# A depthwise-convolution block on one core: image 0's statistics taken alone, its high part formed straight from x, TensorE's ring taps given back to the vector engines

## The reference

```python
xd = jnp.concatenate([x[:, :, 0::2, 0::2], x[:, :, 0::2, 1::2], x[:, :, 1::2, 0::2], x[:, :, 1::2, 1::2]], axis=1)
feats = jnp.concatenate([_dwconv(xd, w1, 1), _dwconv(xd, w3, 3), _dwconv(xd, w5, 5)], axis=1)
y = jnp.einsum('bchw,oc->bohw', feats, w_proj[:, :, 0, 0])
...
x = x + _L0_conv_ref(_gn(x), L0_conv_w1, L0_conv_w3, L0_conv_w5, L0_conv_w_proj)
```

## Time and profile before

| | |
|---|---|
| time, median of 3 runs (lowest, highest) | 147.63 us (145.98, 148.36) |
| the profiled execution's own time | 147.7 us |
| its span, first to last instruction | 145.9 us |
| TensorE busy | 129.1 us (88% of the span) |
| VectorE busy | 119.8 us (82%) |
| ScalarE, POOL busy | 103.0 us (71%), 98.3 us (67%) |
| mean granted TensorE clock | 0.979 |

### The profile page before, as it was taken

The page is one execution under the profiler, slowest core; times in us unless marked ns, Lnnn a source line. Parts: engine busy times, 40 slices in busy tenths (PEclk is TensorE's granted clock), DMA queues, the critical chain, the costliest instruction groups (busy, mean ns, idle before and its releaser), DMA issues.

```text
span 145.9 us, 1480 instructions
## 1 busy us (share of the span) xinstructions
PE 129.1 (88%) x501; PEld 95.9 (66%) x501; DVE 119.8 (82%) x134; ACT 103.0 (71%) x110; POOL 98.3 (67%) x73
## 2 busy tenths in 40 slices
PE   0374699999999999999999999999999999999910
PEld 0222578788876777678767776777677867776600
DVE  0198999996299999999999999799938995999460
ACT  2285999999955999599959995999599950004100
POOL 7104799999699628994999399829993999100840
PEclk9999879999999999999999999999999999999996
DMA  3999993052043007000708699107094992853966
GB/s 101 216 210 212 209 211 50 0 110 49 0 98 57 0 19 136 0 4 17 136 0 180 122 186 206 38 17 136 0 216 84 174 198 55 180 112 85 196 145 150
DMA packets 35431, 15.73 MB, mean 108 GB/s; under 512 B 34016, under 2 KB 34144, under 8 KB 35040
## 3 DMA queue, kind: packets, MB, share of 16 engines
q1 hardware_dynamic: 33408, 8.39, 31.6%
q0 software_dynamic: 1440, 7.04, 24.9%
...
...
## 4 chain that ended last, share of the span: by engine, by line
PE 85%; DVE 4%; DMA 3%; ACT 2%; ACTq 1%; issue 1%; DVEq 1%; POOL 0%; POOLq 0%
PE YP L551 75%; PE YP L594 9%; DMA w_sb<-in_L_conv_w_dram 3%; DVE st L424 2%; DVE X L522 1%; ACT G L340 1%; DVE weff L449 1%; DVEq L86 0%; ACT HI L384 0%; PE SMALL L533 0%; POOL rstd L253 0%; ACTq L312 0%; ACTq L311 0%; PE SMALL L539 0%; ACTq L310 0%
## 5 line engine op out<-in xcount | busy, mean ns | idle before, releaser
L275 POOL TENSOR_TENSOR RING_SUM<-RING_SUM,PROD 128x900 f32<-128x900 f32 (+1 forms) x37 | 75.2, 2034 | 7.7 <-ACT PROD L365 3.8
L489 DVE SCALAR_TENSOR_TENSOR ACC<-G,coef,ACC 128x930 f32<-128x930 f32 (+1 forms) x64 | 76.6, 1197 | 2.0
L551 PE MATMUL YP<-HI,whi 128*128 128x512 f32 (+1 forms) x150 | 39.1, 413 | 2.8 <-ACT HI L384 2.8
L551 PE MATMUL YP<-LO,whi 128*128 128x512 f32 (+1 forms) x150 | 40.4, 420 | 0.0
L551 PE MATMUL YP<-HI,wlo 128*128 128x512 f32 (+1 forms) x150 | 37.7, 402 | 0.0
L551 PEld LDWEIGHTS YP<-HI,whi 128*128 128x128 f32 x150 | 29.5, 197 | 11.0 <-DVE whi L468 3.4
L365 ACT ACTIVATE PROD<-G,coef 128x900 f32<-128x900 f32 (+1 forms) x37 | 36.2, 1053 | 0.0
L551 PEld LDWEIGHTS YP<-LO,whi 128*128 128x128 f32 x150 | 28.5, 190 | 10.0 <-issue 3.4
L551 PEld LDWEIGHTS YP<-HI,wlo 128*128 128x128 f32 x150 | 28.3, 190 | 7.1
L375 ACT ACTIVATE Y<-YP 64x1024 f32<-64x1024 f32 x14 | 15.3, 1096 | 24.1 <-PE YP L594 23.9
L340 ACT ACTIVATE G<-X,nbias,rstd 64x1024 f32<-64x1024 f32 (+2 forms) x18 | 21.9, 1215 | 1.9 <-DVE nbias L442 1.5
...
## 6 DMA issues: line engine op xcount, KB each, us to landing
...
X<-in_x_dram SPq DMA_DIRECT2D x12, 256.0 KB, 5.4
...
out_dram<-X SPq DMA_DIRECT2D x12, 256.0 KB, 5.8
...
w_sb<-in_L_conv_w_dram ACTq DMA_DIRECT2D x1, 12.5 KB, 3.8
```

Source lines behind the costliest of these rows:

```text
L275: pool.tensor_tensor(dst, dst, prod(b, k), ALU.add).then_inc(prod_added, 1)
L489: dve.scalar_tensor_tensor(part(ACC, tap), g_tap(b, tap), of5(tap), part(ACC, tap), ALU.mult, ALU.add).then_inc(acc_step, 1)
L551: mm = nc.tensor.matmul(dst, w[:, n, :], src, start=start, stop=False, skip_group_check=True)
```

## The change

Parts, in the order of the program:

- **x is also loaded in another layout** (XS: each channel's 64x64 cut into 4 parts of 16 rows, one per partition) for images 0 and 1. VectorE takes their statistics from XS (`part_bn`), spreads them with a mask (L485), TensorE sums the four parts by a 0/1 matrix `same` (`sum_parts`), VectorE aggregates (`part_variance`, `part_bias`). Image 0 and image 1 now have statistics of their own; pairs 1 to 3 go as before, at other places of `between`, their powers on POOL at other places too.
- **The high part of image 0 straight from x**: three quarter-to-half pieces on ScalarE (`high_half`, L377), one on VectorE (L547); G follows on ScalarE (L387).
- **Weights in three chunks of three taps**, with (0, 0) last; six taps are scaled on ScalarE, three on POOL (L329); VectorE adds and casts per chunk, POOL forms wlo per chunk (L333). The 3x3 coefficients are loaded through POOL's queue as its first instruction. Zero pads are cleared by VectorE instead of POOL. `coef` is copied by ScalarE.
- **No ring taps on TensorE**: VectorE has 10, 10, 11, 10, ... taps (before 8, 11, 11, 10, ...), POOL's products are 5, 5, 4, 5, ... (before 4, 4, 4, 5, ...).
- **copy_y(b-2) among the products of image b** instead of copy_y(b-3) before the normalisation of image b.
- **Other keep-warm matmuls**: 9 of 128 columns before the transposes, 3 behind them, 8 of 512 columns behind `sum_parts(0)`.

```diff
-EXTRA = [(1, 2), (-1, 2), (1, -2)]
-EXTRA_OF = {0: EXTRA}
 POOL_TAPS = [(0, 2), (-2, -2), (-2, 2), (2, -2), (2, 2), (-2, -1), (2, 1)]
-POOL_N = [5, 5, 5, 6, 6, 6, 6, 6]
+POOL_N = [6, 6, 5, 6, 6, 6, 6, 6]
...
+INV_STD_AT = {(3, 2): 2, (5, 2): 3}
...
-WARM = (2, 2)
+WARM = (9, 3, 8)
+COPY_Y_AT = [0, 0, 0, 1, 3, 3, 3, 3]
...
+        def load_parts(eng, b, c0, c1, s):
+            src = x[b].rearrange("c (k r) w -> (c k) (r w)", k=PARTS)
+            eng.dma_start(XS[:, b, c0:c1], src[:, c0:c1]).then_inc(s, 16)
         @block.sync
         def _(sp):
-            load_x(sp, 0, x_top, 0, PH // 2)
-            load_x(sp, 0, x_loaded[0], PH // 2, PH)
-            for t in range(1, PAIRS):
-                load_x(sp, t, x_loaded[t], 0, PH)
+            load_parts(sp, 0, 0, 512, xs_loaded[0])
+            load_parts(sp, 0, 512, 1024, xs_loaded[1])
+            load_image(sp, 0, image_loaded[0])
...
+            pool.dma_start(w_sb[:, W3_AT:W1_AT], w3.rearrange("c a h w -> c (a h w)")).then_inc(w3_loaded, 16)
...
+            for n in range(ACT_SCALED, N_INNER):
+                pool.tensor_scalar(weff[:, n, :], wpT[:, 2, :], of5(INNER[n]), None, ALU.mult).then_inc(pool_scaled, 1)
+            for k in range(CHUNKS):
+                taps = slice(k * CHUNK, (k + 1) * CHUNK)
+                pool.wait_ge(whi_ready, k + 1)
+                pool.tensor_tensor(wlo[:, taps, :], weff[:, taps, :],
+                                   whi[:, taps, :].bitcast(F32), ALU.subtract).then_inc(wlo_ready, 1)
+            low_image(0)
             inv_std(2, 1, 2)
-            for b in range(1, B):
-                sum_ring(b)
-                if b == 1:
-                    inv_std(3, 2, PAIRS)
+            sum_products(0)
+            low_image(1)
+            inv_std(3, 2, 3)
+            sum_products(1)
...
+            def high_half(r0, r1, j, done):
+                src = X[0:HALF, 0, r0:r1, :].rearrange("p h (w j) -> p h w j", j=2)[:, :, :, j]
+                act.activation(s_image(HI, 0, r0, r1)[HALF * j:HALF * (j + 1)], src, ACT.Identity,
+                               bias=nbias[0:HALF, 0:1], scale=rstd[0:HALF, 0:1]).then_inc(done, 1)
...
+                    if b >= 2 and k == COPY_Y_AT[b]:
+                        copy_y(b - 2)
...
+            high_half(0, TOP, 0, hi_top)
+            high_half(TOP, PH, 0, hi_bottom)
+            high_half(TOP, PH, 1, hi_ready)
+            normalise(0, 0, PH, g_ready)
...
+                dve.wait_ge(part_stats, 2 * b + 3)
+                dve.tensor_tensor(spread[:, b, :, :], stp[:, b, None, :].to_broadcast([P, PARTS, STATS]),
+                                  mask[:, :, None].to_broadcast([P, PARTS, STATS]), ALU.mult).then_inc(spread_done, 1)
+            def part_variance(b):
+                dve.wait_ge(spread_summed, b + 1)
+                dve.bn_aggr(agg1[:, b, :], SPREAD_PS[b]).then_inc(agg1_done, 1)
+                dve.wait_ge(agg1_done, b + 1)
+                dve.tensor_scalar(vare[:, b:b + 1], agg1[:, b, 1:2], EPS, None, ALU.add).then_inc(stat_step, 1)
+            def part_bias(b):
+                dve.wait_ge(rstd_done, b + 1)
+                dve.scalar_tensor_tensor(nbias[:, b:b + 1], agg1[:, b, 0:1], -1.0, rstd[:, b:b + 1],
+                                         ALU.mult, ALU.mult).then_inc(stats_ready, 1)
...
-            between = {(0, 0): lambda: aggregate(1), (0, 2): lambda: (bn(2), aggregate(2)), (0, 3): lambda: variance(2, 1, 2),
-                       (0, 4): lambda: bn(3), (0, 6): lambda: aggregate(3), (0, 5): lambda: bias(2, 1, 2),
-                       (0, 7): lambda: variance(3, 2, PAIRS), (1, 5): lambda: bias(3, 2, PAIRS)}
+            between = {(0, 0): lambda: part_variance(1), (0, 2): lambda: part_bias(1), (0, 3): lambda: bn(1),
+                       (0, 4): lambda: aggregate(1), (0, 5): lambda: variance(1, 1, 2), (0, 6): lambda: bias(1, 1, 2),
+                       (1, 9): lambda: bn(2), (2, 0): lambda: aggregate(2), (2, 5): lambda: variance(2, 2, 3),
+                       (2, 7): lambda: bias(2, 2, 3), (3, 9): lambda: bn(3), (4, 0): lambda: aggregate(3),
+                       (4, 5): lambda: variance(3, 3, 4), (4, 7): lambda: bias(3, 3, 4)}
...
+            for _ in range(WARM[0]):
+                keep_warm(ident[:, :], P)
...
+                nc.tensor.matmul(SPREAD_PS[b], same[:, :], spread[:, b, :, :].rearrange("p k s -> p (k s)"),
+                                 start=True, stop=True).then_inc(spread_summed, 1)
...
+                if b in (0, 2, 4):
+                    t = b // 2 + 1
+                    combine(t, t, t + 1)
...
             for _ in range(WARM[1]):
-                keep_warm()
-            pe.wait_ge(whi_ready, 1)
+                keep_warm(ident[:, :], P)
+            pe.wait_ge(w5_loaded, 16)
+            pe.wait_ge(w3_loaded, 16)
+            coefficients(0, W1_AT, coef_ready)
+            sum_parts(0)
+            pe.wait_ge(low_zero, 1)
+            zeros = LO[:, SLOTS - 1, :]
+            for _ in range(WARM[2]):
+                nc.tensor.matmul(YP[:, 0, 0:512], zeros[:, 0:P], zeros[:, 0:512], start=True, stop=True)
```

More of the change, by code:

```diff
@@ L52 @@
 TOP = BANK_ROWS + 1
-WARM = (2, 2)
+WARM = (9, 3, 8)
+COPY_Y_AT = [0, 0, 0, 1, 3, 3, 3, 3]
+CHUNK = 3
+CHUNKS = N_INNER // CHUNK
+ACT_SCALED = 6
+PARTS = 4
+STATS = 12
+COLS = 2 + PAIRS - 1
 SUMS = 3
@@ L232, in _ @@
                                base=0, pattern=[[-1, P]], channel_multiplier=1).then_inc(const_step, 1)
+            pool.memset(same[:, :], 0.0).then_inc(stat_const, 1)
+            for k in range(PARTS):
+                pool.wait_ge(stat_const, k + 1)
+                v = same[:, :].rearrange("p (n c) -> p n c", c=C)
+                pool.affine_select(out=v, in_=v, compare_op=ALU.not_equal, fill=1.0, base=-k,
+                                   pattern=[[0, P // C], [-PARTS, C]], channel_multiplier=1).then_inc(stat_const, 1)
             a = avg[:, :].rearrange("p (b i c) -> p b i c", b=2, i=2)
@@ L340, in normalise @@
                     act.activation(g_image(b, r0, r1)[HALF * j:HALF * (j + 1)], rows[:, :, :, j], ACT.Identity,
[L341 to L342 removed]
+                                   bias=nbias[p0:p0 + HALF, col(b):col(b) + 1],
+                                   scale=rstd[p0:p0 + HALF, col(b):col(b) + 1]).then_inc(done, 1)
             def split(b):
@@ L452, in _ @@
+            part_bn(0)
+            part_variance(0)
             dve.wait_ge(wpT_ready, 3)
             dve.wait_ge(coef_copied, 1)
-            bn(0, 0, 2)
             add_w3(0, 1, 2)
-            bn(0, 2, 4)
-            aggregate(0)
-            add_w3(3, 4)
-            variance(1, 0, 1)
-            add_w3(5, 6)
-            bias(1, 0, 1)
-            add_w3(7, 8)
-            dve.scalar_tensor_tensor(weff[:, 0, :], wpT[:, 0, :], coef[:, W1_AT:W1_AT + 1],
-                                     weff[:, 0, :], ALU.mult, ALU.add).then_inc(weff_step, 1)
@@ L471, in add_tap @@
+            cast_w(2)
+            part_bn(1)
             def add_tap(b, k):
@@ L525, in _, with keep_warm @@
         def _(pe):
-            pe.wait_ge(const_step, 4)
+            def keep_warm(tile, n):
+                nc.tensor.matmul(YP[:, 0, 0:n], tile, tile, start=True, stop=True)
+            pe.wait_ge(const_step, 3)
+            for _ in range(WARM[0]):
+                keep_warm(ident[:, :], P)
             for k in range(3):
@@ L578, in low @@
                     mm = tap_matmuls(b, n, whi, LO)
-                extra = EXTRA_OF.get(b, [])
-                if extra:
-                    pe.wait_ge(extra_low_ready, 1)
-                for tap in extra:
-                    n = PE_TAPS.index(tap)
-                    tap_matmuls(b, n, whi, HI)
-                    tap_matmuls(b, n, wlo, HI)
-                    mm = tap_matmuls(b, n, whi, LO)
                 mm.then_inc(inner_done, 1)
+                if b in (0, 2, 4):
+                    t = b // 2 + 1
+                    combine(t, t, t + 1)
             def ring(b):
```

261 lines of the change are left out of this document (152 added, 109 removed).

## The result

| | median | range | runs |
|---|---|---|---|
| before | 146.91 us | 145.98 to 148.36 | 4 |
| changed | 148.47 us | 148.16 to 148.97 | 4 |

The ratio is 1.011, 95% interval 1.006 to 1.016: 1.1% slower, more than the noise and less than 2%. The profiled execution took 148.97 us (span 147.2), that of before 147.7. In some executions a kernel falls into a slower state, and every ratio here compares the other executions alone, while the medians are over all.

What follows compares the result with a forecast made beforehand. TensorE bounds the kernel before and gains about 5 us, but the bound moves to VectorE: its ledger puts F(7) at 137.9 and ring(7) at 138.0 instead of 137.23, +0.8 on 147.7, so 148.5 us, range 144.1 to 150.9.

Steps and rivals of the forecast that it cites:

- Case A: The main case, with holds and waits as summed: 148.5 us, with its tails 147.6 to 150.9, chance 0.42.
- The head: Start of the kernel: transposes at 6.6 us, G(0) ready at 16.3, third cast ending at 17.3.
- case D: POOL's weight scalings take t instead of 0.35 us, shifting the first ring tap by 3(t - 0.35); 151.6 at 1.4, chance 0.10.
- case B: Spreading of image 1 gets in before POOL's low part, first ring tap at 18.7 instead of 20.8: 146.4 us, chance 0.20.
- The spreading: VectorE's two-SBUF-input spreading of image 1 starts 0.2 us behind POOL's low part and waits 2.2; first ring tap at 20.8.
- Pair 1's power: POOL has it done at 35.0 us, VectorE asks at 32.6 and waits 2.3; F(0) at 39.6.
- Image 2's first step: VectorE's step meets POOL's first add of image 3: a hold of 0 or 1.9 us, taken as 0; F(2) at 69.5.
- Image 6: VectorE starts image 6 at 112.9 us, 3.4 after F(5), because pair 3's bias comes late; F(7) at 137.9.
- What follows is unchanged: After ring(7), four matmuls, two adds and the last stores take as long as before, so its 0.8 us delay sets the end.
- The copies of Y cost nothing: ScalarE's copies among the products cost nothing, as ScalarE waits for biases anyway; a late copy could take TensorE 1 to 2 us.
- case C: No holds between VectorE and POOL in the head, F(0) 3.6 us earlier: 144.9, or 144.2 with the clock early; chance 0.24.
- VectorE trails TensorE by 1.06 us only: Before the change, F(7) is done at 136.17 and its product starts at 137.23, so TensorE's gain needs VectorE's ring to gain too.

Runs made afterwards that it cites:

- e10: Changed kernel with ScalarE scaling all nine weights and POOL none: 146.56 us, 0.997 of the kernel before.
- e3: Changed kernel with image 1's spreading on ScalarE, as four scaled copies between products of image 0: 146.60 us, 0.992 of the kernel before.
- e2: Changed kernel with each image's spreading as four VectorE instructions of one tensor input instead of one with two: 149.23 us, 1.013 of the kernel before.
- e4: Changed kernel with pair 1's power on POOL behind its fourth product add of image 0: 148.97 us, 1.010 of the kernel before.
- e11: Changed kernel with many follow-up edits together, but pair 1's power at its old place: 142.91 us, 0.973; with that power moved too, 141.06 us.
- e9: Changed kernel with the copies of Y back at their place of before, three images behind: 152.31 us, 1.040 of the kernel before.
- e5: Kernel before with only image 0's ring taps off TensorE, POOL taking one tap more of images 0 and 1: 144.63 us, 0.983.
- e6: Changed kernel with pair 3's statistics, combination and bias earlier: 147.12 us, 0.998 of the kernel before.

## Why the prediction was right, and where it was not

The forecast was 148.5 us in 144.1 to 150.9, and the median is 148.47. Case A happened. So good an agreement is in part luck. The sum was made for the profiled execution, which took 148.97 us, 0.5 over it. That execution was the slowest of the four. The base was off too: the forecast takes 147.63 us for the kernel before, and with its fourth run the median is 146.91. So the change was forecast at 0.6% and measured at 1.1%. Inside the sum two errors of 1.5 us cancel (below).

- **The bound moves to VectorE**: right (chain, and 5.2 us of TensorE's waits for F in all, 2.34 of them before ring(7)).
- **The head**: transposes at 6.96 instead of 6.6 (nine products 4.21 for 4.05, and a start at 2.96 for 2.5); G(0) at 16.5 (16.3); third cast ends at 16.96 (17.3). POOL's scalings took 0.63, not 0.35: a part of case D, whose 3(t - 0.35) is 0.8 us. e10 shows 0.7 for the cast; the other 2.1 of its first ring tap are case B's race, which that edit won through a later G.
- **The spreading**: 2.28 us, ending with POOL's low part, first tap at 20.39 (20.8). e3 shows that the end hangs on it, with 2.8 us; e10, in which the cast came earlier too, gained 2.1. Its explanation was too narrow (e2).
- **Pair 1's power**: wait 2.36 (2.3), F(0) at 39.8 (39.6). That this wait was on the path was true only in the sum, not as a cause: removed alone it gives nothing (e4), removed with the rest 2.2 us (e11).
- **Image 2's first step** is the term of the sum that was mis-sized: taken as 0, it was 1.5, and F(2) was at 71.3 instead of 69.5. I chose by the nearest row, in which VectorE was first. Here POOL's add was first, by 0.53 us (55.26 against 55.79), and the step ended 1.1 us behind that add. The order hung on less than the sum's own error, as it did at the spreading.
- **Image 6**: wait 3.28 (3.4). F(7) at 140.0 instead of 137.9: 1.5 of the hold, the rest in small pieces.
- **"What follows is unchanged"** failed by 1.5 us the other way: the stores no longer stand in line (1.1) and the last one landed sooner. That cancels the hold.
- **"The copies of Y cost nothing"**: they cost nothing at the end, and their new place was worth 4 us (e9). The ledger came out right because I put the copies' new place into TensorE's slack and never asked what the new statistics would do with the old place.
- **The chances** do not add up as given. Half of case C's 0.24 is 0.12, not 0.15, and case B with the clock up early is 145.7, above the 144.7 that "faster" needs, so its 0.05 has no ground. The ends of the range are near, but not at, what the cases give (144.2, and 150.7 with the late clock and the hold).
- **The step that failed** is the one on what bounds the kernel before: that VectorE trails TensorE by 1.06 us only, and the kernel can gain no more than VectorE's ring also gains. VectorE's 5.3 us of waits for POOL and 4.0 for a combination product were not its own. They came from TensorE: conv late, Y copied late, products late, POOL's sum late. Take TensorE's 4 us away and they shrink (e5). So the loss is not in the ring taps, which gain 2.4 us. It is in the rest of the change, 4.1 us by the difference of two ratios. Within it, the statistics of images 0 and 1 alone and pair 3's at a later place bring VectorE a wait of 2.4 and one of 3.3, and put its first tap 2.6 us later, a hold of 2.1 among it. How the 4.1 us divide among them is not shown: removed one by one, three of them give 2.8 (e3), nothing (e4) and 2.0 (e6). The high part straight from x and the weights in chunks were not taken out by themselves.
